# A transformer decoder layer on one core: TensorE's loop over 16 steps with branches, a mask row, 128x64 cross scores, narrower causal matmuls and a new plan

## What is computed

```python
x = x + attn(layernorm(x))          # 16 heads of 16, causal softmax, W_qkv, W_out
x = x + xattn(layernorm(x), ctx, mask)
x = x + ffn(layernorm(x))

def xattn(h, mem, mask):            # one head of 256, keys = values = mem
    s = where(mask, h @ mem.T / 16, -1e30)
    return where(any(mask), softmax(s) @ mem, 0)

def bit_linear(x, w, g):            # of the ffn: 256 -> 2*704, gate*sigmoid(gate)*up, 704 -> 256
    xn = rms_norm(x, g)
    scale = 127 / max(abs(xn))                      # per token
    xq = clip(round(xn * scale), -128, 127) / scale
    s = 1 / mean(abs(w))
    wq = clip(round(w * s), -1, 1) / s
    return xq @ wq.T
```

## Time and profile before

| | |
|---|---|
| median of 3 runs | 234.59 us (234.19 to 235.38) |
| the profiled execution | 235.14 us |
| its span | 233.3 us |
| mean granted TensorE clock | 0.946 |
| busy: PE, DVE, ACT, POOL | 197.4, 170.9, 146.9, 138.4 us |
| instructions | 11731, of them 4512 matmuls and 4512 weight loads |

### The profile page before, as it was taken

One profiled execution on the slowest core, in us unless ns is written; L12 is line 12 of the kernel. 1 busy time (PEld: TensorE's weight loads), 2 busy tenths in 40 slices (PEclk: granted clock), 3 DMA queues, 4 the chain that ended last, 5 costly groups with the idle time before them and its releaser, 6 DMA issues.

```text
span 233.3 us, 11731 instructions
## 1 busy us (share of the span) xinstructions
PE 197.4 (85%) x4512; PEld 155.9 (67%) x4512; DVE 170.9 (73%) x555; ACT 146.9 (63%) x406; POOL 138.4 (59%) x282
## 2 busy tenths in 40 slices
PE   4688769997989899969999999999999998957654
PEld 4576648775768787757878687878787865633332
DVE  2231657896889787848687878787878889998871
ACT  2248654563758686664868676868686759645541
POOL 8850061444857565652738383939383958788980
PEclk9889999999999999997999999999999999985785
DMA  6997000101011010100101010101010101000011
GB/s 174 381 327 233 3 3 6 48 10 45 3 48 49 26 47 28 49 25 3 46 24 46 22 45 22 48 22 45 22 48 22 49 25 49 25 0 1 24 49 45
DMA packets 11545, 12.77 MB, mean 55 GB/s; under 512 B 1072, under 2 KB 10864, under 8 KB 11504
## 3 DMA queue, kind: packets, MB, share of 16 engines
q1 hardware_dynamic: 11440, 12.24, 16.5%
q0 software_dynamic: 64, 0.00, 0.0%
HBM read 10.14 MB, written 2.10 MB: 52 GB/s over the span
## 4 chain that ended last, share of the span: by engine, by line
PE 56%; issue 14%; POOL 14%; DVE 9%; ACT 4%; POOLq 1%; DVEq 0%; ACTq 0%
PE ps L292 9%; PE ps L320 7%; PE ps L286 7%; PE ps L308 6%; PE ps L407 6%; PE ps L343 4%; PE ps L424 3%; POOL m L1662 3%; POOL bh L1666 3%; PE ps L336 3%; DVE o_out L1217 2%; PE ps L435 2%; POOL rs L1565 2%; PE ps L373 2%; PE ps L477 2%
## 5 line engine op out<-in xcount | busy, mean ns | idle before, releaser
L1649 POOL TENSOR_TENSOR zh<-hh,gd 128x352 f32<-128x352 f32 x32 | 30.1, 944 | 35.2 <-DVE hh L1175 35.2
L1040 DVE TENSOR_REDUCE mx<-ps 128x16 f32<-128x1024 f32 x16 | 19.6, 1225 | 22.0 <-PE ps L343 21.8
L308 PE MATMUL ps<-yaT,wqk 128*128 128x128 f32 x256 | 33.3, 284 | 2.6 <-ACT yaT L674 1.4
L308 PEld LDWEIGHTS ps<-yaT,wqk 128*128 128x128 f32 x256 | 30.5, 194 | 4.2 <-ACT yaT L674 2.0
L773 ACT ACTIVATE th_sb<-ps,th 128x352 f32<-128x352 f32 x32 | 17.6, 551 | 17.1 <-issue 14.7
L292 PE MATMUL ps<-wg,zT 128*128 128x352 bf16 x128 | 25.9, 333 | 1.7 <-ACT zT L674 1.6
L1563 POOL TENSOR_SCALAR ve<-mv 128x1 f32<-128x1 f32 x32 | 6.7, 210 | 32.1 <-DVE mv L1087 19.4
L1565 POOL TENSOR_TENSOR rs<-ve,neghalf 128x1 f32<-128x1 f32 x32 | 19.8, 618 | 2.7
L731 ACT ACTIVATE pT<-ps 128x512 f32<-128x512 f32 x32 | 18.4, 596 | 4.7 <-PE ps L379 3.6
L320 PE MATMUL ps<-wv,yaT 128*64 128x128 f32 x256 | 19.0, 288 | 2.0 <-issue 2.0
L674 ACT ACTIVATE hT<-ps 128x512 bf16<-128x512 bf16 (+1 forms) x32 | 15.2, 488 | 6.1 <-PE ps L286 6.1
(11 more groups left out here) (127 smaller groups left out, 524.5 us busy)
## 6 DMA issues: line engine op xcount, KB each, us to landing
ct_in<-ctx_t SPq DMA_DIRECT2D x16, 128.0 KB, 2.1
cn_in<-ctx_n SPq DMA_DIRECT2D x16, 128.0 KB, 2.5
out<-o_out SPq DMA_DIRECT2D x16, 128.0 KB, 1.7
wg<-gate_t SPq DMA_DIRECT2D x1, 1408.0 KB, 7.8
x_in<-x SPq DMA_DIRECT2D x1, 1024.0 KB, 10.8
wd<-down_t SPq DMA_DIRECT2D x1, 640.0 KB, 8.7
wqk<-wqkv_t SPq DMA_DIRECT2D x1, 512.0 KB, 4.0
x_in<-x SPq DMA_DIRECT2D x1, 512.0 KB, 8.7
```

Of the source, the lines that this page charges most:

```text
L308: last = pe.matmul(qk_ps[:, e * P:(e + 1) * P], wqk[:, c, e * P:(e + 1) * P], yaT[:, t % 2, c, :], start=(c == 0), stop=(c == DC - 1))
L1040: V.tensor_reduce(out=mx[:, t % 2, :, :], in_=scores, op=ALU.max, axis=AX).then_inc(ev["mx_d"], 1)
L1649: G.tensor_tensor(zh[:, t % 2, part], hh[:, t % 2, part], gd[:, part], ALU.mult).then_inc(ev[f"zh_d{j}"], 1)
```

## The change

TensorE's straight steps 2 to 5 and 14 to 17 go into the loop, which now has eight turns of two steps, 2 to 17. A step touches tiles that don't exist in the first or last turns (negative, or over 15); `within` puts a branch around such a stage, and around each wait in `freed` whose count lies outside of 1 to 16 in some turn. The stages in a step are in a new order, and the PSUM banks are dealt out anew. The other engines' orders are new and fully unrolled too.

```diff
+TURNS = 8
-        xT_ps = ps[:, 1, 0:D]
-        v_ps = ps[:, 0, 0:D]
-        d_ps = ps[:, 6, 0:D]
+        xT_ps = bank(1, D)
+        v_ps = bank(3, D)
+        d_ps = bank(0, D)
...
+            def within(t, least, most):
+
+                if isinstance(t, int):
+                    return nullcontext()
+                low, high = (least - t.base + 1) // 2, (most - t.base) // 2
+                if low > 0 and high < TURNS - 1:
+                    return pe.If((t.turn >= low) & (t.turn <= high))
+                if low > 0:
+                    return pe.If(t.turn >= low)
+                return pe.If(t.turn <= high) if high < TURNS - 1 else nullcontext()
...
                 for name, count in users:
-                    pe.wait_ge(ev[name], at(count))
+                    with within(count, 1, T) if not isinstance(count, int) else nullcontext():
+                        pe.wait_ge(ev[name], at(count))
...
-                            pe.matmul(psS[SEQ * b:SEQ * (b + 1), g, 0:256].rearrange("p (n k) -> p n k", k=SEQ), pick_bf[rows, half, :],
-                                      causal_bf[rows, half, :].unsqueeze(1).broadcast_to([32, 4, SEQ]),
+                            pe.matmul(psS[SEQ * b:SEQ * (b + 1), g, 0:256].rearrange("p (n k) -> p n k", k=SEQ)[:, :, 32 * half:32 * half + 32],
+                                      late_bf[rows, half, :], ident_bf[rows, rows].unsqueeze(1).broadcast_to([32, 4, 32]),
...
-                pe.matmul(sx_ps[:, :], seq_bf[:, :], mask_bf[:, t if isinstance(t, int) else t.turn * 2 + t.base, :], start=True, stop=False)
+                pe.wait_ge(ev["mask_d"], at(t + 1))
+                seqs = [slice(SEQ * b, SEQ * (b + 1)) for b in range(2)]
+                for rows in seqs:
+                    pe.matmul(sx_ps[rows, :], row_bf, mask_bf[:, t % 2, rows], start=True, stop=False)
                 for c in range(DC):
-                    last = pe.matmul(sx_ps[:, :], yxT[:, t % 2, c, :], ct_in[:, t % 2, c, :], start=False, stop=(c == DC - 1))
+                    for rows in seqs:
+                        last = pe.matmul(sx_ps[rows, :], yxT[:, t % 2, c, rows], ct_in[:, t % 2, c, rows], start=False, stop=(c == DC - 1))
...
+            readout(1, ("oN_d", 1))
+            transpose_yx(0, ("mx_d", 3))
             def step(s):
+                with within(s + 1, 0, T - 1):
+                    transpose_ya(s + 1, ("wmean_set", 1), ("q_d", s + 1), ("k0_d", s + 1), ("k1_d", s + 1), ("zT_d", s - 3))
+                with within(s - 4, 0, T - 1):
+                    gate_up_0(s - 4, ("mx_d", s + 1), ("exp_d1", s), ("exp_d0", s), ("h1_d0", s - 4), ("hh_d0", s - 4))
+                cross_scores(s - 2, ("mx_d", s + 1), ("exp_d1", s), ("expx_d", s - 2))
...
+                with within(s + 1, 0, T - 1):
+                    project_v(s + 1, ("v_d", s + 1), ("h1_d1", s - 3), ("hT_d1", s - 4))
+                    scores_q(s + 1, ("exp_d0", s + 1), ("exp_d1", s + 1))
...
-            with pe.Fori(0, 4) as turn:
-                for base in range(6 - 5, 6 + 4):
+            with pe.Fori(0, TURNS) as turn:
+                for base in range(-3, 6):
                     at(Tile(base, turn))
                 for k in range(2):
-                    step(Tile(6 + k, turn))
+                    step(Tile(2 + k, turn))
...
-                copy(pxT[:, t % 2, :], pxT_ps).then_inc(ev["pxT_d"], 1)
+                for b in range(2):
+                    rows = slice(SEQ * b, SEQ * (b + 1))
+                    last = nc.scalar.activation(pxT[rows, t % 2, rows], pxT_ps[rows, rows], ACT.Copy, scale=2.0)
+                last.then_inc(ev["pxT_d"], 1)
```

More of the change, by code:

```diff
@@ L1 @@
-from contextlib import ExitStack
+from contextlib import ExitStack, nullcontext
 import concourse.bass as bass
@@ L473, in down @@
                 freed(users)
-                if t == 0:
+                if first(t):
                     pe.wait_ge(wd_rdy, 1)
@@ L521, in _ @@
-            cross_readout(0, ("x1_d", 2))
-            transpose_ya(4, ("q_d", 4), ("k0_d", 4), ("k1_d", 4))
-            readout(2, ("expx_d", 1))
-            transpose_yx(1, ("x2_d", 1))
-            scores_q(3, ("exp_d0", 3), ("exp_d1", 3))
-            cross_scores(1, ("oN_d", 3))
-            transpose_readout(2, ("yxT_d", 2))
-            project_qk(4, ("yaT_d", 5))
-            transpose_cross_weights(1, ("mx_d", 4))
-            transpose_max(3, ("mx_d", 4))
-            project_out(2, ("oT_d", 3))
@@ L532, in _ @@
-            scores_k(3, ("mx_d", 4), ("pxT_d", 2), ("mT_d", 4))
-            cross_readout(1, ("x1_d", 3))
-            transpose_z(0, ("v_d", 4))
-            scores_q(4, ("exp_d0", 4), ("exp_d1", 4))
-            gate_up_0(0, ("q_d", 5), ("k0_d", 5), ("k1_d", 5), ("zT_d", 1))
-            readout(3, ("expx_d", 2))
-            transpose_yx(2, ("x2_d", 2))
-            gate_up_1(0, ("mx_d", 5))
-            transpose_ya(5, ("h1_d0", 1))
-            transpose_readout(3, ("yxT_d", 3))
-            cross_scores(2, ("oN_d", 4))
@@ L565, in _ @@
-            cross_readout(3, ("x1_d", 5))
-            scores_k(5, ("hh_d1", 2), ("h1_d1", 2), ("pxT_d", 4), ("mT_d", 6))
-            project_qk(6, ("yaT_d", 7))
-            down(0, ("exp_d1", 6))
-            transpose_z(2, ("v_d", 6))
-            transpose_yx(4, ("x2_d", 4))
-            readout(5, ("hT_d1", 1))
-            scores_q(6, ("exp_d0", 6), ("out_d", 1), ("exp_d1", 6))
-            gate_up_0(2, ("q_d", 7), ("k0_d", 7), ("k1_d", 7), ("zT_d", 3))
-            transpose_readout(5, ("yxT_d", 5))
@@ L669, in _ @@
-            down(15, ("out_d", 15))
+            transpose_h_0(15, ("out_d", 15))
+            down(15, ("hT_d0", 16))
         @block.scalar
@@ new lines, in _ @@
+            normalise_x1(4)
+            keep_zT(2)
+            keep_v(6)
+            keep_yxT(4)
+            normalise_x(8)
+            tanh_0(2)
+            keep_yaT(7)
+            tanh_1(2)
+            cross_exponentials(4)
+            keep_oT(5)
+            normalise_x(9)
+            keep_max(6)
+            squares_0(2)
+            keep_cross_weights(4)
+            keep_k_0(7)
+            keep_k_1(7)
+            keep_hT_1(1)
+            keep_q(7)
+            exponentials_0(6)
@@ new lines, in _ @@
+            exponentials_1(6)
+            keep_hT_0(1)
+            squares_1(2)
+            keep_v(7)
+            normalise_x1(5)
+            keep_zT(3)
+            keep_yxT(5)
+            keep_yaT(8)
+            tanh_0(3)
+            tanh_1(3)
+            cross_exponentials(5)
+            normalise_x(10)
+            keep_oT(6)
+            keep_k_0(8)
+            keep_cross_weights(5)
+            keep_max(7)
+            keep_k_1(8)
+            keep_hT_1(2)
+            keep_q(8)
```

1389 lines of the change are left out of this document (863 added, 526 removed).

## The result

The changed kernel takes 365.05 us (median of 4 runs, 363.8 to 365.3) where the kernel before takes 234.94 on the same chip (4 runs, 234.2 to 235.4): 1.553 times as long, with a 95% interval from 1.547 to 1.559. The prediction was 279 us with a range to 350. The sign, the engine and the bound by its instruction queue were right, the size was not: 130 us were added, and I had worked out 44.

A forecast was written before the change was run, and what follows sets the result against it. TensorE's instruction queue was to bound the loop. Entry at 30 us, turn 0 26.7, turn 1 29.4, turns 2 to 6 149, turn 7 22 and end 19.5 give 276.6; with 1.8 around it, 279 us, range 241 to 350.

The forecast's parts named there:

- a first ya that starts earlier: Front: GpSimd's mask memset and two DMA issues go, so the first ya comes up to 2 us earlier; 1.7 taken.
- The price of a comparison: TensorE's queue in a full step: 49 branches that fall through at 0.135 us, 6.6 us.
- The price of a guarded wait: TensorE's queue in a full step: 47 waits that stand alone at 0.11 us, 5.2 us.
- The rest of the queue's work: Full step: 286 matmul pairs at 0.009 us, 2.6 us of queue; the array's work hides in the queue's.
- a fall inside its range: Full steps: the granted clock may fall where matmuls thin out, costing dense blocks only what the queue doesn't hide.
- the predicted 29.8: Full loop turn of two steps: 14.9 us a step instead of 11.8, turns of 29 to 30 us in the middle.
- the last turn and the end: Turn 7 at 11 us a step, paced by the last tiles' FFN chain, 22 us; then 19.5 us of end.
- Operation per condition: Rival, loop's guards: each comparison first worked out into a register, 0.10 us more per branch, 351 us; chance 0.12.
- Branches hidden: Rival, loop's guards: the queue's spare time covers them behind the array, about 224 us; chance 0.13.
- The fetched loop: Rival: the longer loop body is fetched again each turn, 298 us; chance 0.07, shared with clock at half.
- The estimate by the Trainium skill: Loop's branches at about 108 ns: a step of 13.6 us, the kernel some 17 us faster than forecast.

The follow-up runs named there:

- e5: e3 with wait-guard bounds that always hold, so the build drops the comparisons and leaves 72 closing jumps a turn: 273.5 us.
- e3: e1 with 72 guards a turn around waits alone, all of which hold: 300.2 us, 1.278 times before.
- e10: Changed kernel with half of the loop's readout pairs issued twice, 32 pairs a step more: 365.6 us.
- e12: Changed kernel whose q and k projection in the loop has 8 pairs a step instead of 16: 355.3 us.
- e11: e3 with 27 guarded waits a turn instead of 72, the others unguarded: 248.5 us.
- e9: Changed kernel whose q and k projection in the loop works on 64 of its 128 columns, same instruction count: 369.0 us.
- e2: e1 with the 26 guards a turn around blocks alone, all of which hold: 235.1 us, 0.997 times before.
- e6: Changed kernel with all 64 readout pairs a step issued twice in the loop: 452.7 us.
- e8: Changed kernel with no guards around waits, semaphore starts and last increments raised; 16 steps in the loop and block guards stay: 240.3 us, 1.027 times before.
- e4: Changed kernel with an increment of an unused semaphore behind each guarded wait, so the wait is its own record: 336.0 us.
- e1: Changed kernel without guards: loop of 4 turns, steps 2 to 5 and 14 to 17 straight code: 237.4 us, 1.010 times before.

## Why the prediction was wrong

**Right.** The bound moves from the array to TensorE's instruction queue; 98 comparisons a turn; 10 instruction packets, none of them from 111.9 us on; idle time put down to "issue"; guarded waits that no longer share a record; a first ya that starts earlier (5.7 us forecast, 5.07 measured). Not as foretold are the waits: 20 wait records a turn instead of some 90, the others on jumps and comparisons.

**The price of a comparison** was taken from the loop's branch that falls through, 0.135 us. The record stands at 0.122 to 0.125 where nothing hides it, and e5 bears that out once its additional wait records are counted. So this term was right to about 1 us a turn (98 x 0.011). For the 26 block guards the difference of the changed kernel to e3 gives only 0.07 each.

**The price of a guarded wait** is the step that failed first. "A wait inside its own guard can't be merged: ... 47 x 0.11" took the record of an unguarded wait and forgot that a body of a guard has an end. The wait rides on the jump that closes it, which holds the queue for 0.225 us and not 0.11: 72 x 0.115 = 8.3 us a turn. Nothing in the trace of before showed such a jump, and the sum should have carried the loop's branch (0.21 to 0.24 us plus an interval) as the upper bound of each guard's end. With comparisons at 0.135 and 72 ends at 0.3 it would have reached 43 us a turn.

**The rest of the queue's work** is the second step that failed. "The array's work hides in the queue's, not the reverse", with 572 pairs at 9 ns, makes 5.1 us a turn. The 9 ns were read off a block of matmuls of 32 rows, and for those e10 doesn't contradict it. They were then applied to matmuls of 128 rows, and e12 found some real time behind these. The size of this term isn't measured by itself, but the trace puts it at 5 to 10 us a turn above the 5.1. The lower figure is what is left when guards, waits and register operations of a turn are taken at the distances that they have where they stand alone: 98 x 0.124 + 72 x 0.23 + 20 x 0.11 + 10 x 0.10 = 32 of 42 us. The upper one goes by the starts of the records as they stand in the turn from 111.9 to 153.6 us: 15.4 us lie behind its 572 weight loads, 13.7 behind the closing jumps, 9.6 behind the comparisons and 2.9 behind the rest. The two differ because a load and a guard beside it overlap. The granted clock of 0.83 to 0.92 in such turns may be part of it; the prediction had left a fall inside its range. It does not seem to be most of it: e11's turn, at 1.00, has 15.4 us behind its loads too.

By the lower figure the sum of a full turn closes: the predicted 29.8, less 1 for the comparisons, plus 8.3 for the closing jumps, plus 5 for the rest, is 42.1 us, against 41.1 to 42.7 in the trace. The last of these terms is a remainder, so the sum is bookkeeping and no test. The turns 2 to 6 are 55 of the 87 us that the span differs (turn 6 is shorter, since its late blocks are jumped over). The rest: turn 0 took 37.1 instead of 26.7 and turn 1 40.8 instead of 29.4, which I put down to the same two terms; the loop was entered at 34.0 instead of 30, for two issue waits of 1.4 and 1.7 us and a third projection at a granted clock of 0.50 (3.15 us for 14 pairs) came ahead of it, and this differs between traces of the same front, from 31.4 us in e10 to 35.5 in e9; the last turn and the end took 47.3 instead of 41.5.

**The rivals.** "Operation per condition", 351 us, came nearest in time, and for a reason near to it: an extra instruction per guard, though a jump behind the body and no register operation ahead of the branch. That it lies near the measured 365 is luck. It had 0.12. "Branches hidden" is refuted by e3 and true for e2: the point from which it decides is not a price per branch but a number of guards, some 15 guarded waits a turn by the line through e11 and e3. The fetched loop is e6's. The estimate by the Trainium skill ("Advanced Engine Details and Errata", "Control Flow Timing": a compare-and-branch of about 108 ns) is a little under the 0.122 to 0.125 us of the records' distance. The same section has 51 ns for a branch that always jumps; the closing jump, with a wait on it, is a record of 169 ns here, and no run shows one without a wait.

**What is open.** How much of the 5 to 10 us a turn is the array's time at full clock and how much the lower clock; why e12 gains more in turn 0 than in the four full turns together; why the tail of the new order takes 3 us more than that of before.

## What to carry to other kernels

Price a guard by everything that it puts on the queue: the comparison, the end of its body, and the wait that could have shared a record or ridden on the next load; here 0.35 us together, or 0.30 more than the same wait without a guard, and free only as long as the queue has time to spare. Before a loop swallows its edges with guards, ask for each wait whether it could stand unconditionally, by raising the semaphore's start and its last increment: e8 took back 125 of 130 us that way. And take the price of a matmul pair in the queue from a block of the same shape, since small ones cost it next to nothing (e10) and behind large ones a part of the array's time is added (e12).

## What the runs showed of the hardware that I had not expected

- A guard's body that ends in a wait is closed by a jump that carries it: 169 ns a record, 0.225 to 0.25 us of the queue, against 51 ns and about 0.11 us for a wait's own record. Where an increment follows the wait, the jump is not there at all (e4).
- An unguarded wait ahead of a guard rides on the guard's comparison (37 of the 98 in a turn). Without the comparisons (e5) such waits stand alone: 47 wait records a turn instead of e3's 20.
- A loop of 1472 TensorE records a turn stays loaded, one of 1600 is fetched again in each turn (35 instruction packets in four turns), and costs about 11 us a turn (53 instead of 42), of which 3.7 at the loop's branch. The Trainium skill ("Runtime: NRT & Kernel Launch", "Instruction fetch mechanics") gives 2048 instructions of room; e6 does not bear that out for a loop, as far as records count its instructions, and the measurement decides.
- Half the columns did not shorten a block of 128-row fp32 matmuls (e9: 1.90 and 2.14 us for 16, against 1.95 for the full width in e1 at full clock).
